# A four-layer decoder on one core: identity products at the first layer's and the scan loop's first steps, first expert weights split by GpSimd, and one copy of the sums at the channel switch

## The chip, the cores and the metric

The program runs on one core of a Trainium2 chip. The metric is the device time of one execution in microseconds; lower is better. The engines are named as in the profile: PE is TensorE's matrix product (PEld its weight load), DVE is VectorE, ACT is ScalarE, POOL is GpSimd, SP issues the DMAs.

## What is computed

Eight sequences of 128 tokens of 128 features pass four layers. Each layer is attention, a second mixing stage and an expert (feed-forward) stage, each on a normalised copy of the tokens and added to them:

```python
# layer 0: rotary causal attention (16 heads of 8), "depool", relu experts (8, two chosen)
# layer 1: banded attention on x itself, dense 128-512-128, context attention, gelu experts
# layer 2: a state-space scan, wide cross attention with the context, 8 experts with 3-valued weights
# layer 3: packed-qkv attention, "depool", 8 gated experts
def _mamba_forward(...):
    def step(s, inp):
        dA_t, dBu_t, C_t = inp
        s = dA_t * s + dBu_t
        y_t = jnp.einsum('bdn,bn->bd', s, C_t)
        return (s, y_t)
    ...
    residual = jnp.einsum('bdn,d->bd', s_final, D)
    y = y + residual[:, None, :]
    y = y * _silu(res)
```

## The kernel before

Everything is one launch, with an instruction stream written by hand for each engine and joined by semaphores; a `Share` counts the events of one stage. The order of the work is the order of the calls in the five engine functions at the end of `decoder`: nothing is moved by a scheduler.

Tokens stand on the 128 partitions, 8 blocks of 128 (`k.x`). A norm is statistics and a variance on DVE (`token_stats`, `variance`), a power on POOL (`Norm.power`, 128x4), and four subtract-and-scale operations on DVE per half of the blocks (`Norm.normal`, L135). `Turn` transposes a half on PE (L181) and ACT copies it out of PSUM (L194) as `xnT`.

`Attention` runs 16 steps, two for each block. In step s PE forms the scores of step s+2 (L346 or L344 for the mask, L352), transposes the weights of step s (L361), and multiplies the weights of step s-1 with the values (L384); DVE takes maxima (L514) and copies transposed weights out of PSUM (L522), ACT exponentiates (L683), POOL makes the next block's keys. Later steps turn outputs back (L400), normalise them (L532, L533), in two of the four kinds transpose and project them (L408, L413), and add them to the tokens (L545). `tail` is a callback with the step's number past 16, in which the next stage's work is woven in. Four stages are such attentions: "rope", "self", "context" and "packed".

`Experts` keeps the tokens and the first weights as sums of two rounded parts, because a product of rounded values takes fewer passes: `split` is a cast (L969) and a subtraction (L970) of 128x512. `first_weights` splits the weights of experts 0 and 1 (of the dense layer the only one), `split_x` a half of the tokens. L850 are the products of the first layer, L915 the nonlinearity, L870 the second layer's products, L995 the weighted sum.

`Mamba` scans 2 channels x 16 states in 32 steps. In a step PE spreads the rows of B and C over the partitions (L1318, L1330), DVE multiplies (L1456) and scans (L1464), ACT makes the decay (L1426) and copies C (L1434), POOL multiplies states and C (L1530), and PE adds the product to the sums in PSUM by an identity product (L1343, `sum_up`). After 16 steps the sums of the first channel are copied out of PSUM so that the second channel can use the banks (`sums_out`, the channel switch).

`spin` issues products of the identity with itself into a bank that nobody reads:

```python
def spin(k, pe, bank, n):
    for _ in range(n):
        pe.matmul(k.ps[:, bank, 0:P], k.ident, k.ident, start=True, stop=True)
```

## Time and profile before

| what | value |
|---|---|
| median of 3 runs | 1028.01 us (1026.97 to 1032.7; the runs are 1032.7, 1028.01, 1026.97) |
| the profiled execution, its own time | 1033.77 us |
| its span, first to last instruction | 1031.9 us |
| mean granted TensorE clock | 0.982 |
| busy | PE 958.4, PEld 717.0, DVE 616.3, ACT 488.6, POOL 339.1 us |
| POOL's first memsets end, and PE and DVE may start | at 4.53 us |
| rope attention, its loop | about 31 to 92 us |
| relu experts begin | 108.73 us |
| dense layer begins | 277.61 us |
| gelu experts begin | 349.96 us |
| scan loop, first and last scan | 492.69 to 613.5 us |
| gate experts begin | 921.91 us |

A stage's border shows in the table as the first L850 product. The busy shares are averages over stages with different limits; what ends a wait at a border is read from the timeline there.

### The profile page before, as it was taken

The numbers are of one execution on the slowest core, as the hardware profiler recorded it, in microseconds if no ns is written. First come the engines' busy times: TensorE is split into PE (matmuls) and PEld (weight loads), VectorE is DVE, ScalarE is ACT, GpSimd is POOL, SyncE is SP. The second block draws the span as 40 slices with busy tenths as digits, with TensorE's granted clock in tenths as the row PEclk, the third lists the DMA queues.
The fourth block names the chain that finished last, engine by engine and source line by source line (L and its number), as shares of the span: only waits on it lengthen the run. The fifth ranks groups of instructions, "written<-read, shape, count | busy, mean of one in ns | idle before, by whom it ended". The sixth has DMA issues, their size and how long they took to land.

```text
span 1031.9 us, 17543 instructions
## 1 busy us (share of the span) xinstructions
PE 958.4 (93%) x6778; PEld 717.0 (69%) x6778; DVE 616.3 (60%) x1290; ACT 488.6 (47%) x1124; POOL 339.1 (33%) x430
## 2 busy tenths in 40 slices
PE   6998999999889899999898989999989989989998
PEld 3555889975666789984333337777768976678997
DVE  6687725378877652231899886544666367862221
ACT  1664434446525554444656544443434447624443
POOL 3751299744167000010466753222210026210000
PEclk9899999999999999999798999999999999999999
DMA  5700011100010011003000001000000000000111
GB/s 127 210 2 11 1 41 42 31 21 2 1 42 1 12 42 42 31 2 122 1 0 0 1 0 42 1 2 1 1 1 1 1 1 2 2 12 25 38 41 31
DMA packets 32134, 25.50 MB, mean 25 GB/s; under 512 B 3564, under 2 KB 28337, under 8 KB 31796
## 3 DMA queue, kind: packets, MB, share of 16 engines
q1 hardware_dynamic: 32051, 24.39, 7.9%
q8 instruction: 54, 0.88, 0.3%
q14 instruction: 29, 0.23, 0.1%
HBM read 23.85 MB, written 0.52 MB: 24 GB/s over the span
## 4 chain that ended last, share of the span: by engine, by line
PE 69%; DVE 21%; issue 4%; ACT 3%; POOL 2%; SPq 0%; DMA 0%; DVEq 0%; POOLq 0%; ACTq 0%
PE banks L870 20%; PE banks L850 14%; DVE work L1464 6%; PE banks L361 4%; PE banks L352 3%; DVE banks L1456 3%; PE banks L1672 3%; PE banks L1664 3%; DVE work L522 2%; PE banks L384 2%; PE banks L1686 2%; PE banks L1723 2%; PE banks L1711 1%; PE banks L1343 1%; PE banks L1654 1%
## 5 line engine op out<-in xcount | busy, mean ns | idle before, releaser
L915 ACT ACTIVATE work<-banks,keep 128x512 f32<-128x512 f32 x236 | 157.0, 688 | 182.3 <-PE banks L850 182.2
L870 PEld LDWEIGHTS banks<-keep,work 128*128 128x128 f32 x1888 | 222.0, 193 | 6.4 <-ACT work L915 1.2
L870 PE MATMUL banks<-keep,work 128*128 128x128 f32 x1888 | 223.3, 276 | 0.9 <-ACT work L915 0.8
L995 DVE SCALAR_TENSOR_TENSOR keep<-banks,keep 128x128 f32<-128x128 f32 x256 | 72.1, 343 | 194.5 <-PE banks L870 194.2
L850 PE MATMUL banks<-rounded 128*128 128x512 f32 x672 | 171.3, 401 | 3.3 <-DVE rounded L970 2.6
L850 PEld LDWEIGHTS banks<-rounded 128*128 128x128 f32 x672 | 121.4, 189 | 30.1 <-DVE rounded L970 4.0
L683 ACT ACTIVATE work<-banks,work 128x128 f32<-128x128 f32 (+1 forms) x448 | 121.6, 389 | 32.6 <-DVE work L514 26.7
L149 POOL TENSOR_TENSOR keep<-keep 128x4 f32<-128x4 f32 x26 | 26.9, 1033 | 271.8 <-DVE keep L128 231.6
L1530 POOL TENSOR_TENSOR work<-work,keep 128x1024 f32<-128x1024 f32 x31 | 73.4, 2367 | 75.1 <-DVE work L1464 68.8
L514 DVE TENSOR_REDUCE work<-banks 128x8 f32<-128x1024 f32 (+1 forms) x64 | 69.0, 1078 | 35.3 <-PE banks L352 32.2
L361 PE MATMUL banks<-keep,work 128*128 128x128 f32 (+1 forms) x448 | 64.4, 285 | 10.7 <-DVE work L522 10.5
L1464 DVE TENSOR_TENSOR_SCAN work<-work,banks 128x1024 f32<-128x1024 f32 x32 | 73.2, 2286 | 1.6 <-ACT work L1426 0.5
L522 DVE COPY work<-banks 128x1024 f32<-128x1024 f32 (+1 forms) x64 | 69.3, 1083 | 5.9 <-PE banks L361 5.6
L1343 PE MATMUL banks<-work,keep 128*128 128x512 f32 x128 | 69.3, 666 | 3.7 <-ACT work L1386 1.8
L361 PEld LDWEIGHTS banks<-keep,work 128*128 128x128 f32 (+1 forms) x448 | 49.4, 144 | 30.6 <-issue 27.1
L1587 POOL TENSOR_TENSOR work<-work 128x968 f32<-128x968 f32 x16 | 29.0, 1814 | 103.5 <-DVE work L1775 103.5
L1828 ACT ACTIVATE work<-banks,work 128x121 f32<-128x121 f32 x128 | 34.2, 380 | 50.1 <-PE banks L1697 45.2
L352 PE MATMUL banks<-rounded 32*128 32x512 f32 (+1 forms) x384 | 56.3, 402 | 1.1 <-POOL rounded L610 0.6
L610 POOL TENSOR_TENSOR rounded<-rounded,keep 128x512 fp32r<-128x512 f32 (+1 forms) x56 | 50.7, 926 | 2.2
L1343 PEld LDWEIGHTS banks<-work,keep 128*128 128x128 f32 x128 | 23.1, 201 | 34.6 <-issue 29.7
L352 PEld LDWEIGHTS banks<-rounded 32*128 32x128 f32 x384 | 29.9, 187 | 24.0 <-issue 19.7
L1456 DVE TENSOR_TENSOR banks<-banks,work 128x1024 f32<-128x1024 f32 x32 | 39.4, 1232 | 8.2 <-PE banks L1318 5.1
(277 smaller groups left out, 1401.4 us busy)
## 6 DMA issues: line engine op xcount, KB each, us to landing
keep<-in_L_ffn_w_dram SPq DMA_DIRECT2D x32, 256.0 KB, 3.0
keep<-in_L_ffn_W_dram SPq DMA_DIRECT2D x16, 256.0 KB, 3.0
keep<-in_L_xattn_Wkv_dram SPq DMA_DIRECT2D x1, 2048.0 KB, 8.2
keep<-in_L_ffn_expert_w_dram SPq DMA_DIRECT2D x8, 128.0 KB, 2.4
keep<-in_L_ffn_expert_w_dram SPq DMA_DIRECT2D x1, 1024.0 KB, 6.6
keep<-in_L_attn_conv_w_dram SPq DMA_DIRECT2D x1, 1024.0 KB, 7.8
keep<-in_ctx_dram SPq DMA_DIRECT2D x1, 960.0 KB, 8.0
keep<-in_x_dram SPq DMA_DIRECT2D x2, 256.0 KB, 3.1
```

The source lines that it names most:

```text
L352: m = pe.matmul(o, q[p][g, :], kb[p][g, 0:self.per, 0:self.T], start=not mask and j == 0, stop=j == 2)
L361: t = pe.transpose(k.ps[0:self.T, PT0 + j // 4, j % 4 * P:(j % 4 + 1) * P], k.pair[s % 2][:, j, 0:self.T], k.ident)
L522: dve.tensor_copy(k.pT[s % 2][0:self.T, :, :].rearrange("t h q -> t (h q)")[:, 0:n], k.ps[0:self.T, PT0:PT0 + 2, :].rearrange("t u n -> t ...
L683: e = act.activation(k.pair[i][:, j, 0:self.T], k.ps[:, 2 * i + j // self.per, at:at + self.T], ACT.Exp, bias=k.nmx[i][:, j:j + 1])
L850: m = pe.matmul(k.ps[:, c, :], w[:, c * P:(c + 1) * P], x[:, h * HALF:(h + 1) * HALF], start=j == 0, stop=j == len(parts) - 1)
L870: m = pe.matmul(k.ps[:, 4 + n % 2, j * P:(j + 1) * P], k.hT[n % 2][:, c, j * P:(j + 1) * P], w2[c], start=c == 0, stop=c == self.nf - 1)
L915: act.activation(k.hT[n % 2][:, c, :], k.ps[:, c, :], self.func, bias=bias, scale=scale)\
L995: ins = dve.scalar_tensor_tensor(acc[:, t, :], k.ps[:, 4 + n % 2, j * P:(j + 1) * P], k.w[:, 8 * t + e:8 * t + e + 1], acc[:, t, :], ALU.m ...
L1343: m = pe.matmul(k.ps[:, 4 + h, :], k.ident, k.sC[s % 2][:, h * HALF:(h + 1) * HALF], start=n == 0, stop=n == self.N - 1)
L1456: dve.tensor_tensor(k.dbu, k.ps[:, 0:2, :].rearrange("p a n -> p (a n)"), k.du[:, s // self.N, :], ALU.mult)\
L1464: dve.tensor_tensor_scan(k.s[s % 2], k.dA[s % 2].rearrange("p b t -> p (b t)"), k.dbu, 0.0, ALU.mult, ALU.add).then_inc(self.scanned.sem, 1)
L1530: pool.tensor_tensor(k.sC[s % 2], k.s[s % 2], k.cb[s % 2], ALU.mult).then_inc(self.sc_ready.sem, 1)
```

## The change

Six edits, all of order or of engine; nothing else is computed.

1. **Identity products.** Seven more ahead of the first transpositions of the program, two ahead of each half of the rope projections, four after the rope attention's counts, three, four and five between the first spreads of the scan loop. At four borders there are fewer (6 to 2, 10 to 3, 11 to 3, 9 to 6).
2. **First expert weights.** `first_weights` is called on POOL, inside the attention that precedes, between the two powers of the next norm, after the wait for the first half's normal. DVE no longer splits them.
3. **Edges.** The eight comparisons of `vector_edges` move from ahead of the keys to behind the first maximum.
4. **Tails.** In "self" and "context" attention the transpositions of the next norm's first half and their copy move one step earlier (to other banks); DVE's `split_x` moves to step 16, behind that step's residual. In the last attention the pooled products and the depool's first half move behind the last output product. In both depool stages `split_x(0)` stands ahead of the second half's statistics, and in the last one the first normal stands ahead of the second half's sum.
5. **Channel switch.** `sums_out` is one copy of 128x1024 instead of eight of 128x128 with a bias; the bias, the scaled last states, is added by POOL in step 19, and POOL's gate product moves from step 19 to step 22.
6. `y_read` counts two events, so that PE waits for the copy alone.

```diff
@@ -259,6 +259,7 @@
         self.scores(pe, 1)
         if self.setup:
             self.setup.tensor_counts(pe)
+            spin(k, pe, PT0, 4)
         if self.kind != "rope":
             spin(k, pe, PT0, 3)
             self.turn.tensor_half(pe, 1, PT0, 2)
...
@@ -283,7 +284,7 @@
                     self.back(pe, (s - 3) // 2)
             elif self.proj and s >= 4:
                 self.turn_outputs(pe, (s - 4) // 2)
-            if tail is not None and s >= self.STEPS:
+            if tail is not None and s >= self.STEPS - 1:
                 tail(pe, s - self.STEPS)
 
     def project(self, pe):
...
@@ -295,6 +296,7 @@
             if h:
                 self.turn.tensor_half(pe, 1)
                 pe.wait_ge(*self.setup.idxT_ready.upto(1))
+            spin(k, pe, 6 if h else 5, 2)
             pe.wait_ge(*self.turn.xT_ready.upto(h + 1))
             for j, w in enumerate(k.l0_qk):
                 pe.matmul(k.ps[:, 4 * h + j, :], w, k.xnT[:, h * HALF:(h + 1) * HALF], start=True, stop=True)\
...
@@ -438,6 +439,8 @@
             self.keys(dve, 1)
         src = k.r if self.kind == "self" else k.x
         self.maxima(dve, 0)
+        if self.setup:
+            self.setup.vector_edges(dve)
         if self.kind != "rope":
             self.norm.normal(dve, 1)
         self.maxima(dve, 1)
...
@@ -449,12 +452,12 @@
                 self.maxima(dve, s + 2)
             if s == 1 and self.kind == "packed":
                 self.keys_half(dve, 1)
-            if tail is not None and s >= self.STEPS:
-                tail(dve, s - self.STEPS)
             if s % 2 == 0 and 4 <= s <= self.STEPS + 2:
                 self.outputs_normal(dve, (s - 4) // 2)
             if s % 2 == 0 and s >= late:
                 self.residual(dve, (s - late) // 2)
+            if tail is not None and s == self.STEPS:
+                tail(dve)
             if s < self.STEPS:
                 self.turned_weights(dve, s)
             if s == 0 and self.setup:
...
@@ -587,6 +591,9 @@
             self.setup.pool_counts(pool)
         self.values_of(pool, B - 1)
         after.power(pool, 0)
+        pool.wait_ge(*self.s_done.upto(self.STEPS))
+        pool.wait_ge(*after.xn_ready.upto(4))
+        first.first_weights(pool)
         after.power(pool, 1)
 
     def query_key_parts(self, eng, c, b):
...
@@ -963,22 +970,22 @@
             if done is not None:
                 done(dve, n)
 
-    def split(self, dve, v, high, low, at):
+    def split(self, eng, chain, v, high, low, at):
 
         cols = slice(at, at + HALF)
-        self.k.dchain.link(dve.tensor_copy(high[:, cols], v[:, cols]))
-        return dve.tensor_tensor(low[:, cols], v[:, cols], high[:, cols].bitcast(F32), ALU.subtract)
-
-    def first_weights(self, dve):
+        chain.link(eng.tensor_copy(high[:, cols], v[:, cols]))
+        return eng.tensor_tensor(low[:, cols], v[:, cols], high[:, cols].bitcast(F32), ALU.subtract)
+
+    def first_weights(self, pool):
 
         for e in (0, 1) if self.routed else (1,):
-            self.split_w1(dve, e)
-
-    def split_w1(self, dve, e):
+            self.split_w1(pool, self.k.pchain, e)
+
+    def split_w1(self, eng, chain, e):
 
         k, p = self.k, e % 2
-        dve.wait_ge(*self.w1_loaded[p].upto(16 * (e // 2 + 1)))
-        self.split(dve, k.w1[p], k.w1_high[p], k.w1_low[p], 0).then_inc(self.w1_split[p].sem, 1)
+        eng.wait_ge(*self.w1_loaded[p].upto(16 * (e // 2 + 1)))
+        self.split(eng, chain, k.w1[p], k.w1_high[p], k.w1_low[p], 0).then_inc(self.w1_split[p].sem, 1)
 
     def add(self, dve, n, acc):
         k = self.k
...
@@ -1235,8 +1236,10 @@
         for s in range(2):
             pe.wait_ge(*self.delta_ready.upto(3))
             self.spread_b(pe, s)
+            spin(k, pe, 5, 4 if s else 0)
             pe.wait_ge(*self.delta_ready.upto(4))
             self.spread_c(pe, s)
+            spin(k, pe, 5, 5 if s else 3)
         for s in range(self.steps):
             if s + 2 < self.steps:
                 self.spread_b(pe, s + 2)
...
@@ -1379,13 +1382,10 @@
 
         k = self.k
         j = k.col["ssm_d"]
+        act.wait_ge(*self.y_done.upto(self.N))
+        act.activation(k.yg[:, 0, :], k.ps[:, 4:6, :].rearrange("p a n -> p (a n)"), ACT.Copy).then_inc(self.y_read.sem, 1)
         act.wait_ge(*self.last_summed.upto(1))
-        k.achain.link(act.activation(k.s_last[:, 0, :], k.s_last[:, 0, :], ACT.Copy, scale=k.cols[:, j:j + 1]))
-        act.wait_ge(*self.y_done.upto(self.N))
-        for b in range(B):
-            t = act.activation(k.yg[:, 0, b * P:(b + 1) * P], k.ps[:, 4 + b // 4, b % 4 * P:(b % 4 + 1) * P], ACT.Identity,
-                               bias=k.s_last[:, 0, b:b + 1])
-        t.then_inc(self.y_read.sem, 1)
+        act.activation(k.s_last[:, 0, :], k.s_last[:, 0, :], ACT.Copy, scale=k.cols[:, j:j + 1]).then_inc(self.y_read.sem, 1)
 
     def scalar_rates(self, act):
         k = self.k
...
@@ -1529,8 +1529,12 @@
             if s < self.steps - 1:
                 pool.tensor_tensor(k.sC[s % 2], k.s[s % 2], k.cb[s % 2], ALU.mult).then_inc(self.sc_ready.sem, 1)
             if s == self.N + 3:
-                pool.wait_ge(*self.y_read.upto(1))
+                pool.wait_ge(*self.y_read.upto(2))
+                v = k.yg[:, 0, :].rearrange("p (b t) -> p b t", t=S)
+                k.pchain.step(pool.tensor_tensor(v, v, bcast(k.s_last[:, 0, :], 2, S), ALU.add))
+            if s == self.N + 6:
                 pool.wait_ge(*self.gate_ready.upto(4))
+                k.pchain.settle()
                 pool.tensor_tensor(k.yg[:, 0, :], k.yg[:, 0, :], k.gate[:, 0, :], ALU.mult).then_inc(self.yg_ready.sem, 1)
 
 
...
@@ -1914,6 +1918,7 @@
     def tensor_first(self, pe):
         k = self.k
         k.arrived(pe, "first")
+        spin(k, pe, 5, 7)
         k.arrived(pe, "l0")
         for j in range(6):
             t = pe.transpose(k.ps[:, 6 + j // 4, j % 4 * P:(j % 4 + 1) * P], k.w_raw[:, j, :], k.ident)
...
@@ -2576,9 +2581,9 @@
 
         def depool_first(pe, j):
 
-            if j == 0:
+            if j == 1:
                 t13.tensor_half(pe, 0)
-            if j == 1:
+            if j == 3:
                 l3_cross.tensor_pooled(pe)
                 l3_cross.tensor_half(pe, 0)
 
...
@@ -2596,16 +2601,16 @@
             k.arrived(pe, "gates")
             spin(k, pe, OB, 10)
             l0_ffn.tensor(pe, tail=lambda pe: t3.tensor_half(pe, 0))
-            l1_attn.tensor(pe, tail=lambda pe, j: t4.tensor_half(pe, 0) if j == 0 else None)
-            spin(k, pe, 0, 6)
+            l1_attn.tensor(pe, tail=lambda pe, j: t4.tensor_half(pe, 0) if j < 0 else None)
+            spin(k, pe, 1, 2)
             l1_dense.tensor(pe)
             l2_mamba.tensor_taps(pe)
             pe.wait_ge(*setup.keyrow.upto(1))
             pe.wait_ge(*l2_mamba.taps_ready.upto(2))
             spin(k, pe, MB, 12)
             t6.tensor_half(pe, 0)
-            l1_cross.tensor(pe, tail=lambda pe, j: t7.tensor_half(pe, 0) if j == 0 else None)
-            spin(k, pe, 0, 10)
+            l1_cross.tensor(pe, tail=lambda pe, j: t7.tensor_half(pe, 0) if j < 0 else None)
+            spin(k, pe, 1, 3)
             l1_ffn.tensor(pe, tail=lambda pe: t8.tensor_half(pe, 0))
             bits.tensor(pe)
             t8.tensor_half(pe, 1)
...
@@ -2618,10 +2623,10 @@
             l2_ffn.tensor(pe, tail=lambda pe: t12.tensor_half(pe, 0))
             k.arrived(pe, "l3")
             l3_attn.tensor(pe, tail=depool_first)
-            spin(k, pe, 2, 11)
             t13.tensor_half(pe, 1)
+            spin(k, pe, 2, 3)
             l3_cross.tensor_half(pe, 1)
-            spin(k, pe, 2, 9)
+            spin(k, pe, 2, 6)
             t14.tensor_half(pe, 0)
             spin(k, pe, 2, 6)
             l3_ffn.tensor(pe)
...
@@ -2680,16 +2677,17 @@
             l0_cross.add(dve, 1)
             n2.normal(dve, 0)
             setup.vector_pooled(dve, 1)
+            l0_ffn.split_x(dve, 0)
             token_stats(k, dve, k.x, range(4, 8))
             n2.variance(dve, 1)
             k.arrived(dve, "gates")
-            l0_ffn.vector_start(dve)
+            l0_ffn.vector_start(dve, split_first=False)
             bits.vector(dve)
             l0_ffn.vector(dve, n3, done=beside_relu)
-            l1_attn.vector(dve, n4, tail=lambda dve, j: dense_first(dve) if j == 2 else None)
+            l1_attn.vector(dve, n4, tail=lambda dve: l1_dense.split_x(dve, 0))
             l1_dense.vector_start(dve, split_first=False)
             dense_sums(dve)
-            l1_cross.vector(dve, n7, tail=lambda dve, j: gelu_first(dve) if j == 2 else None)
+            l1_cross.vector(dve, n7, tail=lambda dve: l1_ffn.split_x(dve, 0))
             l1_ffn.vector_start(dve, split_first=False)
             l1_ffn.vector(dve, n8)
             n8.normal(dve, 1)
...
@@ -2702,12 +2700,17 @@
             l2_after.add(dve, 1, n11)
             l2_ffn.vector_start(dve, split_first=False)
             l2_ffn.vector(dve, n12, last=l3_attn.first_parts)
-            l3_attn.vector(dve, n13, tail=lambda dve, j: l3_ffn.first_weights(dve) if j == 1 else None)
+            l3_attn.vector(dve, n13)
             n13.normal(dve, 1)
-            for h in range(2):
-                l3_cross.vector_half(dve, h, n14)
+            l3_cross.add(dve, 0)
+            token_stats(k, dve, k.x, range(4))
+            n14.variance(dve, 0)
             n14.normal(dve, 0)
-            l3_ffn.vector_start(dve)
+            l3_cross.add(dve, 1)
+            l3_ffn.split_x(dve, 0)
+            token_stats(k, dve, k.x, range(4, 8))
+            n14.variance(dve, 1)
+            l3_ffn.vector_start(dve, split_first=False)
             l3_ffn.vector(dve)
 
         @block.scalar
...
@@ -2741,7 +2744,7 @@
             t11.scalar_half(act, 0)
             l2_ffn.scalar(act)
             t12.scalar_half(act, 0)
-            l3_attn.scalar(act, tail=lambda act, j: t13.scalar_half(act, 0) if j == 0 else None)
+            l3_attn.scalar(act, tail=lambda act, j: t13.scalar_half(act, 0) if j == 1 else None)
             t13.scalar_half(act, 1)
             t14.scalar_half(act, 0)
             l3_ffn.scalar(act)
```

On PE, at the head of the scan loop (`MATMUL ... L1318` and `L1330` are the spreads of B and C, `L1343` the sums), there stood:

```order
L1309 MATMUL banks<-work,keep 128x512 x2
L1318 MATMUL banks<-rounded 128x512 x2
L1330 MATMUL banks<-rounded 128x512 x2
L1318 MATMUL banks<-rounded 128x512 x2
L1330 MATMUL banks<-rounded 128x512 x2
L1318 MATMUL banks<-rounded 128x512 x2
L1330 MATMUL banks<-rounded 128x512 x2
L1343 MATMUL banks<-work,keep 128x512 x2
```

and now, where L1321, L1333 and L1346 are the same lines and L41 is `spin`:

```order
L1312 MATMUL banks<-work,keep 128x512 x2
L1321 MATMUL banks<-rounded 128x512 x2
L1333 MATMUL banks<-rounded 128x512 x2
L41 MATMUL banks<-keep 128x128 x3
L1321 MATMUL banks<-rounded 128x512 x2
L41 MATMUL banks<-keep 128x128 x4
L1333 MATMUL banks<-rounded 128x512 x2
L41 MATMUL banks<-keep 128x128 x5
L1321 MATMUL banks<-rounded 128x512 x2
L1333 MATMUL banks<-rounded 128x512 x2
L1346 MATMUL banks<-work,keep 128x512 x2
```

Three groups of identity products stand between the first four spreads.

On PE, from the last value product of the last attention to the gate experts, there stood (L408 and L413 are the transposition and the projection of an output, L400 its way back, L1085 the pooled products, L1092 the depool products):

```order
L400 MATMUL banks<-keep,work 128x128 x2
L1085 MATMUL banks<-keep 128x512 x2
L1092 MATMUL banks<-keep 128x128 x4
L41 MATMUL banks<-keep 128x128 x3
L408 MATMUL banks<-keep,work 128x128
L41 MATMUL banks<-keep 128x128 x3
L413 MATMUL banks<-keep,work 128x128
L41 MATMUL banks<-keep 128x128 x11
L181 MATMUL banks<-keep 128x128 x4
L1092 MATMUL banks<-keep 128x128 x4
L41 MATMUL banks<-keep 128x128 x9
L181 MATMUL banks<-keep 128x128 x4
```

and now (L410, L415, L402, L1092 and L1099 are those lines):

```order
L402 MATMUL banks<-keep,work 128x128 x2
L181 MATMUL banks<-keep 128x128 x4
L41 MATMUL banks<-keep 128x128 x3
L410 MATMUL banks<-keep,work 128x128
L41 MATMUL banks<-keep 128x128 x3
L415 MATMUL banks<-keep,work 128x128
L1092 MATMUL banks<-keep 128x512 x2
L1099 MATMUL banks<-keep 128x128 x4
L181 MATMUL banks<-keep 128x128 x4
L41 MATMUL banks<-keep 128x128 x3
L1099 MATMUL banks<-keep 128x128 x4
L41 MATMUL banks<-keep 128x128 x6
```

The last output (L410, L415) stands ahead of the pooled products and the first half's depool.

On DVE, from the last attention's last normal to the gate experts, there stood (L135 is a norm's normal, L1105 the depool's sum, L969 and L970 the split):

```order
L135 TENSOR_SCALAR keep<-keep 128x128 x4
L1105 TENSOR_TENSOR keep<-keep,banks 128x512
L160 BN_STATS keep<-keep 128x6 x4
L163 BN_AGGR keep<-keep 128x2 x4
L128 TENSOR_SCALAR keep<-keep 128x4
L1105 TENSOR_TENSOR keep<-keep,banks 128x512
L160 BN_STATS keep<-keep 128x6 x4
L163 BN_AGGR keep<-keep 128x2 x4
L128 TENSOR_SCALAR keep<-keep 128x4
L135 TENSOR_SCALAR keep<-keep 128x128 x4
L969 CAST rounded<-keep 128x512
L970 TENSOR_TENSOR rounded<-keep,rounded 128x512
```

and now (L1106, L976 and L977 are those lines):

```order
L135 TENSOR_SCALAR keep<-keep 128x128 x4
L1106 TENSOR_TENSOR keep<-keep,banks 128x512
L160 BN_STATS keep<-keep 128x6 x4
L163 BN_AGGR keep<-keep 128x2 x4
L128 TENSOR_SCALAR keep<-keep 128x4
L135 TENSOR_SCALAR keep<-keep 128x128 x4
L1106 TENSOR_TENSOR keep<-keep,banks 128x512
L976 CAST rounded<-keep 128x512
L977 TENSOR_TENSOR rounded<-keep,rounded 128x512
L160 BN_STATS keep<-keep 128x6 x4
L163 BN_AGGR keep<-keep 128x2 x4
L128 TENSOR_SCALAR keep<-keep 128x4
```

The normal of the first half and the split of its tokens stand ahead of the second half's statistics; four rows of weight splits (L969, L970, twice) that stood further up are gone from DVE.

## Rows read from the trace of the kernel before

**Rows 1.** The profile page: shares of the chain that ended last.

```profile
PE 69%; DVE 21%; issue 4%; ACT 3%; POOL 2%; SPq 0%; DMA 0%; DVEq 0%; POOLq 0%; ACTq 0%
```

**Rows 2.** Windows: stretch, PE, PEld, DVE, ACT, POOL busy, granted clock, DMA, GB/s.

```profile
30.00:39.00 9.00, 9.00 (x49) 5.92 (x50) 4.85 (x6) 4.74 (x19) 7.47 (x14) 0.50 0.60 169
494.00:507.00 13.00, 11.46 (x18) 4.61 (x17) 11.54 (x7) 7.19 (x11) 7.07 (x3) 0.50 0.00 1
```

**Rows 3.** Timeline, first 24 us: start, us, engine, line, out<-in, count, idle before.

```profile
7.12 1.51 PE L1919 MATMUL banks<-keep,work 128*128 128x128 f32 x6 [7.12 <-DMA work<-in_L_xattn_W_in_dram]
...
10.26 2.04 PE L300 MATMUL banks<-keep 128*128 128x512 f32 x2 [0.78 <-ACT keep L194]
...
14.53 1.66 DVE L1998 TENSOR_SCALAR keep<-work 120x128 bf16<-120x128 f32 x8 [2.52 <-ACT work L1943]
...
20.70 1.02 PE L300 MATMUL banks<-keep,work 128*128 128x512 f32 x2
...
21.11 1.29 DVE L610 TENSOR_TENSOR rounded<-rounded,keep 128x512 fp32r<-128x512 f32 x2
```

**Rows 4.** Timeline, the first attention's transpositions of weights.

```profile
31.50 1.97 PE L361 MATMUL banks<-keep,work 128*128 128x128 f32 x8
...
40.64 1.09 PE L361 MATMUL banks<-keep,work 128*128 128x128 f32 x8
```

**Rows 5.** Timeline, the scan loop's first scans.

```profile
500.01 2.29 DVE L1464 TENSOR_TENSOR_SCAN work<-work,banks 128x1024 f32<-128x1024 f32 x1
...
509.51 2.29 DVE L1464 TENSOR_TENSOR_SCAN work<-work,banks 128x1024 f32<-128x1024 f32 x1
...
513.17 2.29 DVE L1464 TENSOR_TENSOR_SCAN work<-work,banks 128x1024 f32<-128x1024 f32 x1
```

**Rows 6.** Timeline, the channel switch.

```profile
558.11 2.18 ACT L1386 ACTIVATE work<-banks,keep 128x128 f32<-128x128 f32 x8
...
560.43 2.47 PE L1343 MATMUL banks<-work,keep 128*128 128x512 f32 x4 [1.76 <-ACT work L1386]
560.80 2.29 DVE L1464 TENSOR_TENSOR_SCAN work<-work,banks 128x1024 f32<-128x1024 f32 x1
...
574.58 2.29 DVE L1464 TENSOR_TENSOR_SCAN work<-work,banks 128x1024 f32<-128x1024 f32 x1
```

**Rows 7.** Timeline, last attention to gate experts.

```profile
909.32 0.27 PE L408 MATMUL banks<-keep,work 128*128 128x128 f32 x1
...
912.95 1.11 DVE L135 TENSOR_SCALAR keep<-keep 128x128 f32<-128x128 f32 x4 [1.13 <-POOL keep L149]
...
918.54 1.11 DVE L135 TENSOR_SCALAR keep<-keep 128x128 f32<-128x128 f32 x4
...
920.71 0.43 DVE L969 CAST rounded<-keep 128x512 fp32r<-128x512 f32 x1 [1.05 <-ACT keep L194]
...
921.91 3.02 PE L850 MATMUL banks<-rounded 128*128 128x512 f32 x12 [0.53 <-DVE rounded L970]
```

**Rows 8.** POOL's groups by form: count, busy us, mean ns, idle before.

```profile
L1161 POOL TENSOR_TENSOR keep<-keep 128x512 f32<-128x512 f32 x2 | 2.5, 1270 | 3.6 <-DVE rounded L970 3.6
```

**Rows 9.** Timeline, first attention to relu experts.

```profile
91.92 0.25 DVE L532 RECIPROCAL work<-banks 128x16 f32<-128x16 f32 x1
...
105.91 0.60 ACT L194 ACTIVATE keep<-banks 128x512 f32<-128x512 f32 x1 [1.12 <-PE banks L181]
...
108.73 3.02 PE L850 MATMUL banks<-rounded 128*128 128x512 f32 x12 [0.62 <-DVE rounded L970]
```

**Rows 10.** Timeline, context attention to gelu experts.

```profile
346.98 0.60 ACT L194 ACTIVATE keep<-banks 128x512 f32<-128x512 f32 x1 [0.52 <-PE banks L181]
...
349.96 5.74 PE L850 MATMUL banks<-rounded 128*128 128x512 f32 x24 [0.56 <-DVE rounded L970]
```

**Rows 11.** Timeline, DVE at the dense layer's end.

```profile
290.62 4.24 DVE L1136 SCALAR_TENSOR_TENSOR keep<-keep 128x128 f32<-128x128 f32 x4
...
301.25 1.13 DVE L1136 SCALAR_TENSOR_TENSOR keep<-keep 128x128 f32<-128x128 f32 x4
```

40 lines of the change are left out of this document (14 added, 26 removed).

## Prediction

> **What bounds the kernel now.** I read the chain that ended last first: it is mostly TensorE work, with a fifth on VectorE [rows 1]. The chain is one relay through twelve stages, so a local microsecond at a stage's border is worth a microsecond at the end, but one in the middle of an expert layer, where TensorE is full, is worth nothing. Then I read the windows for the granted clock: in the first attention and in the first steps of the scan loop it stands at 0.50, which is the 1.2 GHz level, with TensorE 9.00 of 9.00 us and 11.46 of 13.00 us busy [rows 2]. The reader is to see that a full TensorE there is a slow one. Last I read the timelines at the places that the diff touches.
>
> **The start (identity products ahead of the first transpositions and ahead of each projection half).** The reader is to see the rate in the durations: a pair of half products of 128x512 takes 2.04 us at 10.26 and 1.02 us at 20.70 [rows 3]. The granted clock is not printed low there, but the durations are those of 1.2 GHz and then of 2.4 GHz. TensorE has done nothing until 7.12, where it waited for a weight. The first half's four products fill 10.26 to about 16.8, 6.6 us; at the fast rate they would take 3.7, which is 2.9 less. Seven identity products at a quarter of a 512-column product each (0.43 us slow, 0.21 fast) are 3.0 us, begin with the constants at about 4.6 and end at 7.6: the real work starts 0.5 late. They put TensorE to work 2.5 us sooner and, with the two ahead of the projection, leave no gap of note, so the rate should rise near 8 to 11 us instead of near 15.6. VectorE must follow. Its eight edge comparisons (1.66 us at 14.53) stood ahead of the four key products and now stand in a wait after the first maximum; from their end at 16.2 to the end of the key blocks at 22.40 is 6.2 us [rows 3]. The last two key products and what follows take about 5.1 of these, and would start when the fourth projection is there, about 14.2, so the blocks end at 19.3: **3.1 gained** (bounds: 0.5 lost if only the delay is felt, 4.0 gained).
>
> **The slow stretch in the first attention.** Eight transpositions take 1.97 us at 31.50 and 1.09 at 40.64, and between the two lie two loop steps in 9.14 us [rows 4]. Half of that, 4.6, is the ceiling, and zero the floor if the clock falls as before. The exponentials (2.2 us each step) and VectorE's two 1.2 us operations, with extra context statistics, hold part of it; replaying the waits I get **3.3**. The change puts four identity products (0.9) into the thin part ahead of it. They run ahead of the third score product and delay it by some 0.3, which the next exponentials absorb.
>
> **The scan loop's first steps.** A step's pace is VectorE's, 3.66 us (509.51 to 513.17); from 500.01 to 509.51 two steps take 9.50, 2.18 too much [rows 5], in the stretch at 0.50 [rows 2]. Three, four and five identity products (2.6 us together) stand in waits on ScalarE and VectorE that are each over half a microsecond; each group should end before its successor is released. **2.2 gained**, bounds 0.5 lost and 2.2.
>
> **The channel switch.** Eight ScalarE operations take 2.18 us and the first sum product of the new channel waits 1.76 for them [rows 6]. Now one 128x1024 copy, 1.0 us by the like copies of the loop, does it, and the addition of the last states goes to GpSimd. The product starts about 1.4 sooner, and ScalarE is free before the next scan ends. From 560.80 to 574.58 three steps take 13.78, against 10.98 at the pace: 2.8 lost [rows 6]. I count 2.8 less 0.4 for an additional GpSimd pass of about 2.4 us, which makes the sC products 1.1 late for a step or two; their users have slack of about 0.5 there. **2.4 gained** (bounds 0.5 to 2.8).
>
> **The first expert weights on GpSimd, and the earlier tails.** Per weight VectorE spent a cast and a subtraction, with hand-over 1.2 us (920.71 to 921.91) [rows 7]. On GpSimd a subtraction or product of 128x512 takes 1.27 [rows 8]; the cast is between VectorE's 0.43 [rows 7] and that, I take 0.8, as it reads one input. A pair is 2.1 us, two are 4.2. Ahead of them GpSimd idles; behind them is queued the norm's second power, and VectorE's second normal waits for that.
> - *First attention into depool.* The two pairs, 2.1 us, stood ahead of the last head outputs at 91.92 [rows 9]; these go back to their own release, 1.7 sooner, of which the transposed outputs' ScalarE queue leaves 1.1. GpSimd runs from about 89.9 to 94.1 and the last variance comes at about 94.2: just hidden. At the expert layer's start the split of x now precedes the last four statistics: xT is there at 106.51, plus 1.2 is 107.7 against 108.73 [rows 9]; but the second half's normal then comes 1.3 later in its queue, so half of it stays. **1.6.**
> - *Banded attention into the dense layer.* One pair goes; the second half's normal is the next wait. **0.5.**
> - *Context attention into the gelu layer.* Three pairs stood in a row; now one. xT at 347.58 plus 1.2 is 348.8, and its transpositions, one place earlier in TensorE's order, take off another 0.4, against 349.96 [rows 10]. **1.6.** Fewer identity products (3, not 10) no longer cover this wait, but it is also shorter.
> - *Last attention into depool and the gate layer.* Before, the pooled products and the first half of the depool stood ahead of the last turned output at 909.32 [rows 7]. Moved behind the last output product, they free it: I get it at 905.9, the second normal at 909.7 instead of 912.95 (GpSimd's 903.9 to 908.1 just hidden), with eleven identity products fewer. Then the next norm's first normal is no longer behind the second half's sums and statistics: 913.9 instead of 918.54; the split of x, 920.71 before, follows at 916.0, so the gate layer starts at 917.2 instead of 921.91 [rows 7], 4.7; its second normal now comes later in the queue and takes back 0.5. **4.2.**
>
> **A rule against it.** Four VectorE operations of 128x128 with both inputs in SBUF take 4.24 us at 290.62, while GpSimd works, and 1.13 at 301.25, while it is nearly idle [rows 11]. So GpSimd's new splits can hold up VectorE's residual sums in the banded and context attention, about three operations at up to 1.27, and the mixed splits themselves. I subtract 0.9, half a wait in two places; bounds 0 and 3.8.
>
> The Trainium skill says the same of the port (SBUF — State Buffer, Who interferes with whom): VectorE and GpSimd share one pair as an exclusive lock, which a cast or a two-input operation and a GpSimd operation take in turn, the loser blocked for the whole instruction. By that rule every one of the meetings would cost, and the sum would be smaller by up to 3.8 instead of 0.9; the trace agrees in kind (4.24 against 1.13).
>
> **The sum.** 3.1 + 3.3 + 2.2 + 2.4 + 1.6 + 0.5 + 1.6 + 4.2 - 0.9 = 18.0 us, off the profiled execution's own 1033.77 (span 1031.9): 1015.8. The median of the runs shown is 1028.01, 5.8 below the profiled execution, and one of the three runs, 1032.7, is near it. If the other two were quicker because a slow stretch was missing or shorter, the change gives them less, and the result is 1015.8; if they are quicker for another reason, it is 1010.0. I take the middle, a little low: **1012.5**.
>
> **Rivals.**
> 1. *The clock stays low in the attention and in the scan's first steps* (the identity products fill too little). For it: after the five products TensorE still idles about 1.2 us before the next spread. Against it: the loop's steady steps hold full rate with some idling. Loses 3.3 and 2.2, and 0.5 of delay: 1018.5. Chance 0.22.
> 2. *The ports collide*: pairs on GpSimd take 4 us, both norms' second powers are late by about 4 in the first and last attention. Gives back 1.1 and 3.3 and the 2.9 of the bound: 1020. Chance 0.08. The Trainium skill's rule above would be its cause.
> 3. *More is freed*: the start gains 4.0, the attention 4.6, no collision: 1008 or, from the lower base, 1006. Chance 0.08.
> 4. *It does not do what it says*: each freed wait is replaced by one nearly as late (ScalarE's copies queued at the same tails, the second normal), and the clock stays low: 1025. Chance 0.04.
> 5. *Slower than before*: GpSimd's splits sit ahead of the second power in all four attentions. The cover is about 4.3 us in the first, 4.5 in the last and 8 in the context attention. The other terms are overtaken when the excess over these reaches 18 us, a pair of 5.8 us; near 7 us the kernel would take 1033 or more. A pair of 2.1 from [rows 8] is far off. Chance 0.03.
>
> The forecast itself has 0.55, with 1008 to 1017 as its own range. Rivals 1 and 2 carry the upper end to **1021**, rival 3 the lower to **1005**. A change under 0.5% of the median (5.1 us) cannot be told from none. Above it, faster: the forecast and rivals 1, 2, 3, **0.93**; within: rival 4, **0.04**; slower: **0.03**.
>
> **What the profile after would show.** The 512-column products of the first half in pairs of 1.02; transpositions of 1.1 us in the third and fourth attention step; granted clock 1.00 in the scan loop, scans 3.66 apart from the first to the last, but for a step at the switch; POOL casts of about 0.8 ahead of the second power; the gate layer's first products about 4.7 nearer to the last head output. I would be wrong if the clock still fell, if POOL's cast were as slow as 3 us, or if a DMA that the start now reaches sooner became the wait.

## The result, and the profile after

The changed kernel took 1019.86 us by the median of 11 executions (1017.42 to 1025.45); the kernel before took 1031.91 on the same chips (11 executions, 1026.97 to 1033.07). The ratio is 0.9902, with a 95% interval of 0.9879 to 0.9926: 10 us faster, 7.6 to 12.5. Predicted were 1012.5, in a range of 1005 to 1021. One of before's 78 executions on record, 1051.07 us at a granted clock of 0.919, was in a slow state of its own and is left out everywhere. The direction, the places and most of the mechanisms were right; the time was forecast 7.4 us too low.

The profiled execution took 1017.75, 16.0 less than before's 1033.77. The profile page, its span and its chain that ended last (before: [rows 1]):

```profile
span 1015.6 us, 17561 instructions
PE 68%; DVE 22%; issue 4%; POOL 3%; ACT 2%; DVEq 0%; POOLq 0%; ACTq 0%
```

It is the same relay. The windows (stretch, busy us of PE, PEld, DVE, ACT, POOL, granted clock, DMA) that answer to [rows 2], and two that have no counterpart there:

```profile
27.30:41.10 13.80, 13.26 (x133) 8.51 (x132) 12.02 (x17) 10.25 (x39) 11.83 (x24) 1.00 0.54 147
487.00:501.00 14.00, 12.28 (x32) 4.78 (x31) 13.55 (x8) 8.29 (x11) 9.16 (x4) 1.00 0.01 1
...
107.00:112.00 5.00, 5.00 (x19) 4.06 (x19) 4.76 (x10) 2.07 (x4) 0.00 (x0) 0.66 0.00 0
909.50:914.00 4.50, 4.50 (x15) 3.56 (x15) 1.32 (x5) 2.45 (x5) 0.00 (x0) 0.62 0.00 0
```

The two old stretches at 0.50 are gone, and two shorter ones that before had at 343 and 561 us. Two new ones of 3.4 us have come, behind the gate products of the relu experts and of the gate experts, where before had none. The timeline of the start and the first attention (start, us, engine, line, names, count), which answers to [rows 3, 4]:

```profile
4.59 3.36 PE L41 MATMUL banks<-keep 128*128 128x128 f32 x14 [4.59 <-POOL keep L2757]
...
10.63 1.02 PE L302 MATMUL banks<-keep 128*128 128x512 f32 x2
...
18.44 1.29 DVE L617 TENSOR_TENSOR rounded<-rounded,keep 128x512 fp32r<-128x512 f32 x2
...
23.18 3.95 DVE L2003 TENSOR_SCALAR keep<-work 120x128 bf16<-120x128 f32 x8
...
24.55 2.50 POOL L501 TENSOR_TENSOR work<-work 128x512 f32<-128x512 f32 x2
...
27.05 1.21 DVE L517 TENSOR_REDUCE work<-banks 128x8 f32<-128x1024 f32 x1
...
36.03 1.21 DVE L517 TENSOR_REDUCE work<-banks 128x8 f32<-128x1024 f32 x1
```

The same two maxima in the timeline of before:

```profile
28.25 1.22 DVE L514 TENSOR_REDUCE work<-banks 128x8 f32<-128x1024 f32 x1 [2.33 <-PE banks L352]
...
40.76 1.22 DVE L514 TENSOR_REDUCE work<-banks 128x8 f32<-128x1024 f32 x1 [0.15 <-PE banks L352]
```

The first products run at the 2.4 GHz level, and the key blocks start 2.67 us sooner (18.44 against 21.11). Then the edge comparisons at their new place take 3.95 us instead of 1.66, beside two 128x512 additions on GpSimd, and the second maximum starts at 27.05 behind them. It started at 28.25 before: 1.5 of the 2.7 are lost again. The fifth maximum stands at 36.03, before at 40.76, 4.73 sooner (the expectations below call it the fourth).

The tails. The timeline from the last head outputs to the relu experts ([rows 9] before; GpSimd's splits beside VectorE's row):

```profile
85.18 0.61 POOL L976 CAST rounded<-keep 128x512 fp32r<-128x512 f32 x1 [3.06 <-issue]
85.42 0.26 DVE L535 RECIPROCAL work<-banks 128x16 f32<-128x16 f32 x1 [0.37 <-PE banks L402]
85.87 1.28 POOL L977 TENSOR_TENSOR rounded<-keep,rounded 128x512 fp32r<-128x512 f32 x1
...
101.78 2.99 PE L857 MATMUL banks<-rounded 128*128 128x512 f32 x12
...
107.37 3.14 PE L857 MATMUL banks<-rounded 128*128 128x512 f32 x8
```

A pair takes 1.9 us, and the reciprocal beside it 0.26, as before's 0.25. The relu experts' first products are 6.95 us sooner. In the second group, eight products take 3.14 us where the twelve of 101.78 take 2.99: the clock falls at 108.1. Behind it the gain stands at 4.9. Of the 2.0 given back, 0.4 is not the clock's: edges_third below, with no stretch here, loses that much too, as the second half's normal comes later.

The scan loop's first scans and the channel switch ([rows 5, 6] before):

```profile
491.65 2.29 DVE L1464 TENSOR_TENSOR_SCAN work<-work,banks 128x1024 f32<-128x1024 f32 x1
...
495.31 2.29 DVE L1464 TENSOR_TENSOR_SCAN work<-work,banks 128x1024 f32<-128x1024 f32 x1
...
547.25 1.01 ACT L1386 ACTIVATE work<-banks 128x1024 f32<-128x1024 f32 x1
...
548.41 1.95 PE L1346 MATMUL banks<-work,keep 128*128 128x512 f32 x4 [0.28 <-ACT work L1386]
...
550.26 2.29 DVE L1464 TENSOR_TENSOR_SCAN work<-work,banks 128x1024 f32<-128x1024 f32 x1
...
561.24 2.29 DVE L1464 TENSOR_TENSOR_SCAN work<-work,banks 128x1024 f32<-128x1024 f32 x1
```

Scans stand 3.66 apart from the first on, and from 550.26 to 561.24 three steps take 10.98 at the switch, where before took 13.78. The last attention's way to the gate experts ([rows 7] before):

```profile
892.21 0.30 PE L410 MATMUL banks<-keep,work 128*128 128x128 f32 x1
...
895.87 1.11 DVE L135 TENSOR_SCALAR keep<-keep 128x128 f32<-128x128 f32 x4 [1.12 <-POOL keep L149]
...
900.23 1.12 DVE L135 TENSOR_SCALAR keep<-keep 128x128 f32<-128x128 f32 x4 [1.12 <-POOL keep L149]
...
902.46 0.43 DVE L976 CAST rounded<-keep 128x512 fp32r<-128x512 f32 x1 [0.53 <-ACT keep L194]
...
903.67 3.03 PE L857 MATMUL banks<-rounded 128*128 128x512 f32 x12 [0.60 <-DVE rounded L977]
```

The gate experts start 18.24 us sooner; the shift ahead of this tail was 13.25, so the tail gave 5.0. At 910, 2.0 of them are given back, 1.6 for the stretch and 0.4 as above, and the span is 16.3 shorter.

### The profile page after: what moved, and what is told of

The parts are those of the page before. It is cut to its first block, busy times and chain, and to the rows that moved or that the text cites. A ratio compares the mean times of both kernels' runs of the same rounds, so it can differ in the third digit from the quotient of the medians.

```text
span 1015.6 us, 17561 instructions
## 1 busy us (share of the span) xinstructions
PE 949.8 (94%) x6788; PEld 714.1 (70%) x6788; DVE 613.1 (60%) x1276; ACT 486.4 (48%) x1117; POOL 354.2 (35%) x445
## 4 chain that ended last, share of the span: by engine, by line
PE 68%; DVE 22%; issue 4%; POOL 3%; ACT 2%; DVEq 0%; POOLq 0%; ACTq 0%
PE banks L877 20%; PE banks L857 15%; DVE work L1464 7%; DVE banks L1456 4%; PE banks L363 3%; PE banks L354 3%; PE banks L1676 3%; PE banks L1668 3%; DVE work L525 2%; PE banks L41 2%; PE banks L386 2%; PE banks L1690 2%; PE banks L1727 2%; PE banks L1715 2%; DVE work L517 1%
## 5 line engine op out<-in xcount | busy, mean ns | idle before, releaser
L857 PE MATMUL banks<-rounded 128*128 128x512 f32 x672 | 174.6, 407 | 1.8 <-DVE rounded L977 1.1
L857 PEld LDWEIGHTS banks<-rounded 128*128 128x128 f32 x672 | 123.6, 192 | 29.1 <-issue 3.1
L363 PE MATMUL banks<-keep,work 128*128 128x128 f32 (+1 forms) x448 | 62.2, 279 | 11.2 <-DVE work L525 10.9
L1346 PE MATMUL banks<-work,keep 128*128 128x512 f32 x128 | 63.7, 619 | 2.8 <-POOL work L1530 1.8
L41 PE MATMUL banks<-keep 128*128 128x128 f32 x344 | 47.0, 284 | 6.3 <-POOL keep L2757 4.6
L41 PEld LDWEIGHTS banks<-keep 128*128 128x128 f32 x344 | 43.6, 198 | 10.5 <-issue 5.1
```

What stands on the lines that cost most here:

```text
L363: t = pe.transpose(k.ps[0:self.T, PT0 + j // 4, j % 4 * P:(j % 4 + 1) * P], k.pair[s % 2][:, j, 0:self.T], k.ident)
L857: m = pe.matmul(k.ps[:, c, :], w[:, c * P:(c + 1) * P], x[:, h * HALF:(h + 1) * HALF], start=j == 0, stop=j == len(parts) - 1)
```

## The experiments

Two theories. **A**: each part gives at its place what was forecast, and the rest is lost to the collision at the edge comparisons and to stretches at 0.50 that lie elsewhere from one execution to the next. **B**: the parts give less than forecast, above all since GpSimd's splits hold VectorE up, or the identity products don't hold the clock. In what follows a gain is a start in before's trace less the start of the same instruction in the trace at hand.

**The change in three parts.** The first takes the kernel before and adds

```diff
+            spin(k, pe, PT0, 4)              # behind the counts, first attention
...
+            spin(k, pe, 6 if h else 5, 2)    # ahead of each projection half
...
+            spin(k, pe, 5, 4 if s else 0)    # scan loop, first steps
...
+            spin(k, pe, 5, 5 if s else 3)
...
+        spin(k, pe, 5, 7)                    # start
```

> The kernel before with only the identity products added: 7 at the start, 2 ahead of each projection half, 4 behind the counts in the first attention, 3, 4 and 5 in the scan loop's first steps. The edge comparisons stay where they were. Theory A (each product group raises the clock at its place, the terms of the prediction): granted clock 1.00 in 29 to 39 us and in 487 to 501 us, 3.3 and 2.2 us there, and about 2.5 to 3 at the start; 8 us less than before, 1024 us against 1032. With the comparisons at their old place the second maximum comes at about 25.5 us, not at 27.05 as in the changed kernel, since they then do not meet GpSimd's additions. Theory B (the products only move the slow stretch): a stretch at 0.50 appears elsewhere, the gain is under 4 us: 1028 or more. If the slow stretch of an expert layer's start (108 us in the changed kernel) comes from where the clock's changes happen to fall, it may appear here too and take 1.6 to 2 us of the 8.

Measured: 1025.03 by the median, ratio 0.9941 (0.992 to 0.9962), some 6 us. Both stretches are at 1.00, in windows of its trace:

```profile
27.30:41.10 13.80, 13.03 (x125) 8.26 (x126) 12.29 (x18) 10.98 (x42) 13.12 (x25) 1.00 0.43 121
486.00:508.00 22.00, 19.85 (x66) 9.31 (x66) 20.73 (x14) 14.63 (x19) 11.84 (x5) 1.00 0.01 1
```

The scan's first steps give 2.17, and from the second to the fifth maximum 3.75 are gained. But the start gives only 1.20: with the comparisons at their old place the key blocks wait for them. The second maximum is at 27.05, not at 25.5 as theory A had it, the very time of the changed kernel's first profile. Between these two profiles moving the comparisons brought nothing: what it frees, the collision takes.

The second has only the channel switch (`sums_out` with one copy, the addition on GpSimd).

> The kernel before with only the channel switch changed: one 128x1024 copy on ScalarE in place of eight scaled ones, the addition of the last states on GpSimd, the gate product three steps later. Theory A: the step at the switch is 2.4 to 2.8 us shorter, the rest as before: 2.5 us less, 1029.5 against 1032, and the slow stretch of 561 to 568 us, which lies in that step, gone. Rival: the stretch at 0.50 there has another cause than ScalarE's wait, stays, and the gain is under 1.5 us.

Measured: 1032.62, ratio 1.0009 (0.9992 to 1.0026). In its trace the switch is 2.45 us shorter, and the stretch that lay in it is gone; but another has come at the last attention's start. Windows of it, and of before for the second:

```profile
834.00:844.00 10.00, 8.88 (x49) 7.29 (x50) 4.69 (x16) 3.07 (x4) 1.60 (x7) 0.83 0.01 2
561.00:569.00 8.00, 7.59 (x19) 2.92 (x19) 7.62 (x6) 4.75 (x8) 5.11 (x3) 1.00 0.00 0
```

```profile
834.00:844.00 10.00, 8.52 (x61) 7.02 (x60) 5.84 (x20) 3.07 (x4) 1.92 (x7) 1.00 0.01 2
561.00:569.00 8.00, 8.00 (x14) 3.05 (x13) 5.60 (x3) 4.85 (x7) 3.45 (x3) 0.57 0.00 0
```

At 836 the gain falls from 0.6 to -1.0. That is not the whole of it: this trace is 1.6 us late from the second maximum on (29.88 against 28.25), where the two programs are still the same, since it has another stretch of 3.4 us at 24 that before's profile lacks. A window of it and of before:

```profile
24.00:28.00 4.00, 3.96 (x20) 3.59 (x18) 1.97 (x3) 0.92 (x2) 2.26 (x3) 0.57 0.30 72
```

```profile
24.00:28.00 4.00, 3.57 (x28) 2.62 (x26) 1.93 (x3) 2.54 (x9) 3.49 (x6) 1.00 0.29 74
```

Without that one its span would be some 0.6 us shorter than before's, by these numbers, and not 1.0 longer. The same kernel again:

> The kernel before with only the channel switch changed, once more: in its first profile the step at the switch was 2.45 us shorter than before, yet its median was 1032.6 against 1031.9. Theory A (2.4 gained at the switch, given back where a low clock stretch comes in sooner or later by chance): a profile in which the first attention has the same 10 us at 0.50 as before shows a span 2.4 less than before's, and by executions of like clock the kernel is about 1 to 2.4 us quicker. Rival (the switch's gain is given back at a fixed place behind it, the gelu or bit experts or the last attention): the stretch of 3.4 us at 836 to 840 us, which before did not have, appears again.

1030.85, ratio 0.9992 (0.9969 to 1.0015), with the same 2.5 gained at the switch, the same 1.6 lost at 836 and the same stretch at 24. The two profiles are alike in all their stretches, though, so they say how the gain is given back, not how often. Nor are the executions of the two runs at a clock of 0.988 to 0.989 quicker than before's (1028.8 to 1030.7 against 1027.2 to 1029.7). The switch by itself brings nothing that can be measured here.

The third has only the tails: first weights on GpSimd, transpositions, splits of x and sums in their new order.

> The kernel before with only the first expert weights' splits moved to GpSimd and the reordered tails of the four attentions; no identity products added, no new switch. Theory A (tails are worth what the prediction gave, without a collision): 1.7 at the relu experts' start, 0.8 at the dense layer, 2.6 at the gelu layer, 5.0 at the gate experts' start, 10 us together or 8 if a slow stretch of an expert layer's start takes 2 back: 1022 to 1024 against 1032. Theory B (the pairs on GpSimd hold up VectorE): residual operations of 1 us and more beside the casts, the sum 3 to 5 us smaller, 1026 or more.

Measured: 1023.75, ratio 0.9915 (0.9885 to 0.9946), the larger part of the whole. In its profile, the slowest of the seven executions (1028.94), the last head outputs of the first attention come 1.7 sooner, of which 0.6 is left behind the relu experts' first products, with 3.4 us at 0.50 on the way (at 98.8); the banded tail gives 0.7; the context attention's tail gives nothing (0.02 ahead of it, -0.02 behind) with 6.8 us at 0.50 in it; the last gives 5.0 less 2 behind the gate products. The scan's first steps, which are unchanged here, are 2.0 quicker with 10.2 us at 0.50 instead of 13.7. Theory B's collision is there once, small: one residual sum takes 0.69 us instead of 0.29, in the context attention, beside a cast on GpSimd. The changed kernel's own trace has two:

```profile
336.51 0.69 DVE L548 TENSOR_TENSOR keep<-keep,work 128x128 f32<-128x128 f32 x1
...
339.90 0.56 DVE L548 TENSOR_TENSOR keep<-keep,work 128x128 f32<-128x128 f32 x1
```

None of the other three attentions has any.

**Where the splits are done.** The changed kernel, with the first weights' splits on VectorE again, behind the last step's first work (the same in all four attentions; the first is shown):

```diff
-        pool.wait_ge(*self.s_done.upto(self.STEPS))
-        pool.wait_ge(*after.xn_ready.upto(4))
-        first.first_weights(pool)
...
+            l0_attn.vector(dve, n1, tail=lambda dve: l0_ffn.first_weights(dve))
...
```

> The changed kernel with the first expert weights' splits back on VectorE, at one place, behind the last step's first work, the rest as changed. Theory A (the split on GpSimd is what frees the tails): relu experts' start 2.1 us later less 0.5 of slack, dense layer 0.8, gelu layer 0.8, gate experts 1.5 later: 3 to 5 us in all, about 1023.5 by the median. Rival (the reordered tails alone make the gain, since VectorE waits there anyway): under 1 us.

Measured: 1026.77 (1020.89 to 1032.18), beside 1019.08 for the changed kernel on the same chip. In its profile the first attention's tail gives 0.5 behind the relu experts' first products, instead of the 1.7 of edges_third, which like it has no stretch there; the banded one nothing instead of 0.7; the last 1.6 instead of 3.0 (both net of a stretch behind the gate products): some 3.4 us from the move to GpSimd alone. The rest of the 7.7 is clock: the executions of like clock, at 0.987 (1023.5 and 1023.6, changed) and at 0.988 (1026.8 to 1027.4, this), differ by some 3.5. (The context attention's tail has 6.8 us at 0.50 here and can't be compared.) The new order by itself frees 0.5 in the first attention, nothing in the banded one and 1.6 in the last.

**The comparisons.** The changed kernel, with `vector_edges` in two pieces of four:

```diff
             dve.tensor_tensor(four(k.terms[h][:, r]), four(k.ps[:, 4 * h + 2 * j + 1, :]),
                               bcast(k.sinT, 1, 4), ALU.mult).then_inc(self.turned_qk.sem, 1)
+            if h == 0 and j == 0 and self.setup:
+                self.setup.vector_edges(dve, 0)
...
         if self.setup:
-            self.setup.vector_edges(dve)
+            self.setup.vector_edges(dve, 1)
...
```

> The changed kernel with its eight edge comparisons in two pieces: four behind the first two key products, where VectorE waits 0.8 us, four behind the first maximum, ahead of GpSimd's additions. Theory A (the comparisons take 3.95 us instead of 1.66 because GpSimd's 128x512 additions run meanwhile, and the second maximum waits for them): four take about 0.8 at either place, the second maximum starts at about 25.6 instead of 27.05, and everything from there to the relu experts is 1.4 us sooner: 1018.4 against 1019.9. Rival (the maximum waits for its score product or for TensorE anyway, or the comparisons are slow at this place without GpSimd too): no difference over 0.4 us at the relu experts.

Measured: 1017.78, ratio 0.9869 (0.9844 to 0.9894). The timeline of its start:

```profile
14.02 0.86 DVE L2005 TENSOR_SCALAR keep<-work 120x128 bf16<-120x128 f32 x4
...
23.44 1.12 DVE L2005 TENSOR_SCALAR keep<-work 120x128 bf16<-120x128 f32 x4
...
24.80 2.50 POOL L503 TENSOR_TENSOR work<-work 128x512 f32<-128x512 f32 x2
25.85 1.23 DVE L519 TENSOR_REDUCE work<-banks 128x8 f32<-128x1024 f32 x1 [1.28 <-PE banks L354]
```

Eight comparisons take 1.98, and the second maximum now waits for its scores, not for VectorE: 1.2 us sooner than in the changed kernel. So the 3.95 are the collision, and the changed kernel's own trace shows it operation by operation. Its line of the comparisons (shortest, median and longest of the eight, in ns):

```profile
L2003 DVE TENSOR_SCALAR keep<-work x8: 273/274/1303, 23.2 to 25.8; 120x128 bf16<-120x128 f32 x8
```

The first six start within 1.3 us. The last two start at 24.61 and 25.83, each 0.06 us behind one of the two additions (24.55 and 25.77), and take 1.30 each, as long as the addition (1.28). The kernel ran three times more:

> The kernel with the edge comparisons in two pieces once more, beside the changed kernel on the same chip. The second maximum and the relu experts came 1.2 and 1.1 us sooner in its first profile. Theory A: 1.2 us by medians of like clock; Theory B: the first run's 2.1 us against the changed kernel's median (1017.78 to 1019.86) was more than that because the two pieces also keep the low stretch out of the first attention; then none of its executions lies above 1021.

> The kernel with the edge comparisons in two pieces, as the base of the two above on the same chip: 1018, no stretch at 0.50 in the first attention, one behind the bit experts' gate products.

> The kernel with the edge comparisons in two pieces, as the base of the two above on the same chip: 1018.

Medians of 1018.12, 1017.3 and 1017.74. All its 23 executions lie between 1015.41 and 1020.14, with a median of 1017.8, 1.8 below the changed kernel's 1019.6. That is more than 1.2 us, and the rest is in the spread.

**The changed kernel's own spread.**

> The changed kernel once more, for another profile and for times beside those of its variants on one chip. Seven of its eleven executions took 1017.4 to 1019.9 us at a mean granted clock of 0.992 to 0.995, four took 1023.5 to 1025.5 at 0.985 to 0.987. Theory A (the identity products hold the clock up in some executions and not in others, since its fall depends on where in the program its changes come): a profile of an execution near 0.986 shows a stretch of 13 us or so at 0.50 in the first attention or at the scan loop's start, as before the change; one near 0.993 shows none there, only single stretches of 3.4 us in thin places, other ones than in the first profile. Rival: these four were disturbed from outside, the stretches are spread evenly or there are none.

> The changed kernel on the same chip: 1019.5 by the median. Of 17 executions so far four took 1023.5 or more at a granted clock of 0.985 to 0.987. Theory A (these are executions in which the first attention still ran 7 to 10 us at 0.50): if the profile is of such a one, the fourth maximum stands at about 39 to 40 us, and not at 36.0; if it is not, at 36 to 38. Rival: the low stretch of such an execution lies somewhere else, at the scan loop's start or in the last attention.

> The changed kernel, one look. Seven of its 23 executions took 1023.5 to 1025.6 us. If this is one: the fourth maximum stands 3 to 4 us later than at 36.0, with 7 to 10 us at 0.50 in the first attention (Theory A); or the low stretch lies elsewhere (rival).

Medians of 1019.08 and 1021.69. Of 23 timed executions 16 lie at 1017.4 to 1019.9 (clock 0.992 to 0.995) and seven at 1023.5 to 1025.6 (0.985 to 0.987). The single execution of after_look1 took 1025.29, at 0.985. Windows of its trace, and its fifth maximum:

```profile
27.30:41.10 13.80, 13.80 (x74) 8.69 (x74) 7.55 (x12) 6.53 (x24) 9.19 (x19) 0.53 0.53 152
...
336.00:352.00 16.00, 12.76 (x93) 9.01 (x93) 12.71 (x40) 7.11 (x16) 6.01 (x7) 0.79 0.07 18
```

```profile
41.34 1.22 DVE L517 TENSOR_REDUCE work<-banks 128x8 f32<-128x1024 f32 x1 [0.34 <-PE banks L354]
```

Almost the whole stretch runs at 0.50, with the identity products in it, and the fifth maximum is later than before's 40.76. Five profiles have the changed program up to here. From the second to the fifth maximum they gain 3.5, 2.1, 1.9, -0.4 (splits_on_vector) and -1.7, with 0, 3.4, 3.4, 10.2 and 13.7 us at 0.50; 1.1 by the mean. The four profiles with before's program up to here all take 12.5 us for it, but three of them (switch_only, switch_again, tails_only) have the stretch at 24 and their second maximum at 29.6 to 30.2. By the means of five and four profiles the second maximum comes 2.4 sooner, and not the 1.2 of the first pair. In the seven profiles with the comparisons in two pieces and the four products there is no stretch, and they gain 3.6 each time. The scan's first steps held 1.00 in all of the fourteen profiles with products there, and gave 2.2.

The kernel with the comparisons in two pieces, without the four products behind the counts (the edit against that kernel):

```diff
             self.setup.tensor_counts(pe)
-            spin(k, pe, PT0, 4)
...
```

> The kernel with the edge comparisons in two pieces, without the four identity products behind the counts in the first attention. Theory A (what held the clock in the attention is that TensorE no longer waits 1.7 us for the comparisons): granted clock 1.00 from 24 to 40 us in most executions without them too, and the median within 1 us of the kernel with them. Theory B (the four products hold it): 7 to 14 us at 0.50 in the first attention again, the fourth maximum 3 to 4 us later, the median 2 to 4 us higher.

Measured: 1019.5 (1016.77 to 1023.56), and in its profile

```profile
27.30:41.10 13.80, 13.80 (x86) 8.21 (x88) 9.10 (x14) 7.15 (x27) 12.22 (x23) 0.63 0.50 138
```

with the fifth maximum 4.7 us later than in edges_third, 3.6 of them behind the second. With the wait closed and no products the clock fell in the one profile taken; with the four products and TensorE waiting 1.65 us for the comparisons ahead of them, as in the changed kernel, it held in one of five; with both it held in seven of seven. By time the difference of 2.2 us is suggestive only.

**Keeping the clock up elsewhere.** First, in the kernel with the comparisons in two pieces, the gate products, widened from 8 columns to 64 by repeats that nobody reads:

```diff
-            m = pe.matmul(k.ps[:, 6, 16 * t:16 * t + R], k.xnT[:, t * P:(t + 1) * P], k.router[self.kind],
-                          start=True, stop=True)
+            m = pe.matmul(k.ps[:, 6, 64 * t:64 * t + n * R].rearrange("s (a r) -> s a r", r=R),
+                          k.xnT[:, t * P:(t + 1) * P], bcast(k.router[self.kind], 1, n), start=True, stop=True)
...
```

> The kernel with the edge comparisons in two pieces, and the expert layers' gate products widened: each multiplies by its 8 gate columns repeated to 64 (12 to 60 in the gelu layer) and writes 64 columns; the repeats are not read. In all ten profiles so far a stretch of 3.4 us at 0.50 stood behind the bit experts' gate products, and in most of them one behind the relu or the gate experts', which take 2 us and move 8 columns each. Theory A (TensorE counts as busy there but does too little, and the clock falls): 16 wider products take the same 2 us, the stretches behind the gate products are gone, and since one costs 1.6 to 2 us at the relu and the gate experts, the median falls 2 to 3.5 us below that of the same kernel without it, to about 1015. Rival (the width does not matter, or the products take longer and hold up the second half): the stretches stay, or the time is the same or 1 us longer.

(A stretch stood behind the bit experts' gate products in nine of the ten profiles, not in all.) Windows of its trace, and of the same kernel with 8 columns (edges_again):

```profile
104.00:112.00 8.00, 8.00 (x58) 7.38 (x59) 6.59 (x14) 3.51 (x6) 0.00 (x0) 1.00 0.00 0
774.00:784.00 10.00, 8.64 (x65) 7.80 (x64) 8.18 (x22) 6.13 (x8) 0.00 (x0) 1.00 0.01 2
908.00:916.00 8.00, 8.00 (x55) 6.93 (x54) 3.45 (x11) 4.68 (x8) 0.00 (x0) 1.00 0.00 0
```

```profile
104.00:112.00 8.00, 8.00 (x47) 7.04 (x45) 6.91 (x13) 3.35 (x5) 0.00 (x0) 0.79 0.00 0
774.00:784.00 10.00, 9.87 (x66) 9.43 (x66) 8.35 (x23) 5.36 (x7) 0.00 (x0) 0.83 0.01 2
908.00:916.00 8.00, 8.00 (x46) 7.02 (x46) 1.34 (x5) 3.01 (x5) 0.00 (x0) 0.79 0.00 0
```

All three stretches are gone; 16 products of the relu experts take 1.96 us, and 1.91 with 8 columns. Yet the median was 1018.82, beside 1017.3 with 8 columns on the same chip: no gain in time. The record shows a part of the reason. Two of the four profiles with 8 columns (edges_third and edges_fourth) have no stretch behind the relu or the gate experts' products either. And the one behind the bit experts', which all four have, costs 0.2 us at most: from that layer to the last attention's first maximum the gain over before, which has it too, changes by -0.1 in the changed kernel with the stretch and by +0.1 in waits_filled (below) without it. So the clock's mean rises where the time does not fall: at 0.993 this kernel took 1019.2 to 1019.4, the one with 8 columns 1017.6 to 1018.3. Whether the wider products cost anything themselves is not shown. Its profile still had 10.3 us at 0.50 at two other waits, at 336 and at 824. These I filled next:

```diff
+            if self.kind == "context" and s in (self.STEPS - 2, self.STEPS):
+                spin(k, pe, 1, 7 if s < self.STEPS else 2)
...
-            l2_ffn.tensor(pe, tail=lambda pe: t12.tensor_half(pe, 0))
+            l2_ffn.tensor(pe, tail=lambda pe: (spin(k, pe, 7, 6), t12.tensor_half(pe, 0)))
...
```

> The kernel with the edge comparisons in two pieces and identity products in three further waits: seven in the 1.9 us wait of the context attention's 15th step and two behind its last, six in the 1.5 us wait ahead of the last attention's first transpositions. In seven of eleven profiles with the reordered tails 6.8 us at 0.50 stood at 336 to 351 us and the context attention's way into the gelu layer then gained nothing against before, while it gained 2.6 to 2.7 where the clock stayed up. Theory A (the terms of the tails are right, and a low stretch cancels them in those executions): no stretch at 332 to 345 and none at 820 to 828, and the median 1 to 2.5 us below the same kernel without them, about 1016. Rival (the products are in the way of the work behind them, or only move the stretch by a step): the same median or 0.5 us more, with a stretch at 336 to 345 still there.

> The same with the widened gate products too. Theory A: no stretch at 0.50 anywhere but at the end, the mean granted clock 0.997 or more, median 1014 to 1015.5, with less spread than any kernel so far. Rival (the widened products cost as much as they save, as their kernel's 1018.8 against 1017.3 hints): 0.5 to 1.5 us above the kernel without them.

(It was six of ten profiles, not seven of eleven.) Measured: 1014.83 and 1014.43, beside 1017.74 for the kernel with neither on the same chip; ratios to before 0.9853 (0.9821 to 0.9885) and 0.9848 (0.9816 to 0.9881). The windows of the context attention's tail, in the kernel with neither and in the one with both:

```profile
336.00:352.00 16.00, 15.50 (x93) 13.40 (x92) 5.78 (x22) 8.82 (x13) 2.13 (x2) 0.79 0.07 18
```

```profile
336.00:352.00 16.00, 15.92 (x116) 13.88 (x109) 8.01 (x28) 10.03 (x15) 2.58 (x3) 1.00 0.06 18
```

Over all 14 profiles with the reordered tails this one gives 2.6 in the six where the clock stays up and nothing in the eight where 6.8 us of it are at 0.50. The profile of filled_wide shows a mean clock of 1.000 over a span of 1011.6. It is the quickest kernel here: 5 us below the changed one's median of 1019.6, and 15.8 below before on the same chip. Between it and waits_filled no difference can be told. Nor do the fillings hold the clock each time: one of the six executions of waits_filled took 1019.86 at 0.988, one of filled_wide 1017.85 at 0.992.

## Why the prediction was right and wrong

The terms, predicted and as the first pair of profiles shows them (gains behind each place less those ahead of it):

| term | predicted | profiles |
|---|---|---|
| start, to the key blocks | 3.1 | 2.7 |
| comparisons beside GpSimd's additions | none | -1.5 |
| slow stretch, first attention | 3.3 | 3.5; 1.1 by the mean of five |
| tail into the relu experts | 1.6 | 1.8 |
| stretch behind the relu gate products | none | -1.6 |
| banded into dense | 0.5 | 0.8 |
| context into gelu | 1.6 | 2.6, or 0 at 0.50 |
| scan loop's first steps | 2.2 | 2.2 |
| channel switch | 2.4 | 2.8 |
| last attention into the gate experts | 4.2 | 4.6 |
| stretch behind the gate layer's products | none | -1.6 |
| splits on GpSimd against the residual sums | -0.9 | -0.7, within the 2.6 of the context attention |

The tails into the relu and gate experts are net of the 0.4 that the later normal takes back. The column of the first pair sums to 16.3, the difference of the spans. Every mechanism that the text worked out from rows was there, and of the six terms from the relu experts' tail on five gave more than forecast and one the same.

**The collision that cost came where the text did not look.** The prediction placed it at the residual sums, where it is 0.7 us and hidden in a tail that gained more than forecast. It cost 1.5 us at the comparisons, which the change moves next to two GpSimd additions; both had their rows in the trace before, and to move an operation is also to move it beside others. The Trainium skill's rule (SBUF — State Buffer, Who interferes with whom), that the two engines take one port pair in turn, is what the trace bears out here: 3.95 us beside the additions, 1.98 away from them. The two comparisons that start just behind an addition last the whole of it. Rival 2 had the rule right and the place and price wrong (a pair takes 1.9, not 4). Rival 3's 1008 is not its own sum: 0.9, 1.3 and 0.9 more off 1012.5 are 1009.4.

**The sum took the slow stretches as fixed.** This is the step that failed: the sum promised 18.0 us, and the medians give 12.1 (1031.91 less 1019.86). The first pair of profiles gives 16.0, because before's profiled execution is 1.9 above its median and the changed kernel's 2.1 below. The text had the attention's 3.3 as certain once the products were in, with "the clock stays low" as a rival of its own at 0.22 that loses everything at once. In fact both happen, in different executions of one program: the attention gained 3.5 in one and lost 1.7 in another, 1.1 by the mean of five. The stretches behind the gate products, 1.6 us each where they occur at the relu and the gate experts, had no term at all. And the tails of context and last attention were costed on TensorE's waits alone, though they end in stretches that can fall to 0.50. The sentence that fewer identity products no longer cover the context attention's wait was in the text, at no price; the stretch that it leaves room for takes all 2.6 that the tail gives, in eight of 14 profiles.

**The base.** The prediction weighed 1015.8, from the profiled execution, against 1010.0, from the median of three, and took 1012.5. Over 77 executions before's median is 1031.91, with a spread of 1026.9 to 1036.2 that goes with the granted clock (0.991 to 0.978). The clocks of the two quick ones of the first three are not on record, but the 16 later ones under 1029 us have 0.986 to 0.991 and those of 1032 to 1034 us 0.979 to 0.985: the quick ones are those with less at 0.50, and the text said itself that the change gives these less. By that reasoning 1015.8 was the number to keep; 3.3 of the 7.4 us were lost there. Of the rest, 2.1 are that the changed kernel's profile (1017.75) is quicker than its median, and 2.0 what its profiled time lies above 1015.8.

What stays open: why 1.6 of the switch's 2.5 us are given back at 836 in both of its profiles, and whether they mostly are; what keeps gates_wide from being quicker; and in how many executions each stretch occurs, for which 18 profiles are few.

## What to carry to other kernels

Where the clock has two levels, a kernel has no single time: compare the mean clock of each execution before subtracting a saving from a median of three, and look in the trace at where the low stretches lie, since one may cost nothing and another all that a tail gives. A saving in a stretch where TensorE works thinly is worth its row only if the clock stays up there, so fill the wait that is left, and close a wait ahead of it, in the same edit; the kernels with the most such waits filled were the quickest here. And when an operation moves, list what the engine that shares its port does at the new place.

## What the runs showed of the hardware

- TensorE's records say busy for 16 gate products of 8 columns in 1.9 to 2.0 us, and the granted clock fell to 0.50 behind 26 of the 48 such groups in 16 profiles. 16 products of 64 columns take 1.96 us (relu experts, gates_wide), and it stayed at 1.00 behind all six groups of gates_wide and filled_wide.
- Where in the program the stretches lie changes from one execution to the next: the first attention, the same up to there, had 0, 3.4, 10.2 or 13.7 us at 0.50. An execution's time follows its mean clock, but not closely: the changed kernel took 1017.4 to 1019.9 at 0.992 to 0.995 (1017.4 and 1019.7 both at 0.993), and 1025.1 to 1025.6 at 0.985.
- A VectorE comparison of 120x128 (SBUF to SBUF) takes 0.27 to 0.28 us, and 1.30 where it starts just behind a GpSimd addition of 128x512.
- GpSimd casts 128x512 in 0.61 us (the prediction took 0.8) and subtracts in 1.27.
